# Workspace rounds of a six-stage transformer kernel: mean squares taken from the layer norm, the ends of two sequences alternating on VectorE, two sequences' final statistics by ScalarE's sums

## The reference, cut to what matters

```python
for _ in range(2):
    logits = _rms(x, norm_pre_w) @ compete_w.T + compete_b      # 16 slots
    vals, idx = jax.lax.top_k(jnp.swapaxes(logits, 1, 2), 4)
    wgt = jax.nn.softmax(vals, axis=-1)
    ...                                                          # gather, write, norm: ws
    q, kk, vv = x @ wq.T + bq, ws @ wk.T + bk, ws @ wv.T + bv    # by 8 heads
    att = jax.nn.softmax(jnp.einsum('blhd,bshd->bhls', q, kk) * scale, axis=-1)
    x_b = ctx @ out_proj_w.T + out_proj_b                        # ctx = att @ vv
    x = _rms(x + x_b, norm_post_w)
...
x = _layernorm(x + _L1_xattn_ref(x, ...))     # fifth
x = _layernorm(x + _L1_ffn_ref(x, ...))       # sixth, with the rounds above
```

## Time and profile before

| | before |
|---|---|
| median of three runs | 2493.07 us |
| profiled execution: its own time | 2491.76 us |
| profiled execution: span | 2490.0 us |
| TensorE, VectorE, ScalarE, GpSimd busy, share of the span | 87%, 57%, 51%, 41% |
| mean granted TensorE clock, share of 2.4 GHz | 0.951 |
| last stage | from 2222.6 us to the end |
| last VectorE instruction, last ScalarE instruction ends | 2482.3, 2485.29 |
| last store issued | 2485.31 |

### The profile page before, as it was taken

How to read it: one execution, slowest core, us unless ns; L and a number is a source line. 1 busy time by engine, 2 the same in 40 slices (tenths; PEclk the granted TensorE clock), 3 DMA queues, 4 the chain that set the end, 5 groups by cost and what they waited for, 6 DMA issues and landing times. The chain is left out here.

```text
span 2490.0 us, 33458 instructions
## 1 busy us (share of the span) xinstructions
PE 2164.6 (87%) x12629; PEld 1546.5 (62%) x12664; DVE 1423.2 (57%) x2130; ACT 1258.6 (51%) x2385; POOL 1017.3 (41%) x726
## 2 busy tenths in 40 slices
PE   5989898968896797787999999999999999977782
PEld 4555555536785666565777777777777777744340
DVE  3656666645555435543566765566556665552637
ACT  3636363633425636544555565556655565541413
POOL 2424252511003202203666666666666666530101
PEclk9999999988997999998999999999999999988796
DMA  3000000010001000002111111111111111020001
GB/s 113 1 1 1 1 1 1 1 64 1 1 1 50 1 1 1 1 2 78 51 51 51 60 51 51 47 47 47 48 51 52 51 51 52 18 70 31 1 1 68
DMA packets 60552, 79.14 MB, mean 32 GB/s; under 512 B 6052, under 2 KB 40228, under 8 KB 60392
## 3 DMA queue, kind: packets, MB, share of 16 engines
q1 hardware_dynamic: 60392, 76.99, 9.3%
HBM read 72.78 MB, written 4.19 MB: 31 GB/s over the span
## 5 line engine op out<-in xcount | busy, mean ns | idle before, releaser
L2133 PE MATMUL banks<-s_probsT,s_v 128*128 128x512 f32 x512 | 230.1, 592 | 0.0
L594 DVE TENSOR_REDUCE s_neg_max<-banks 128x1 f32<-128x512 f32 x256 | 165.5, 685 | 89.4 <-PE banks L660 88.0
L2039 DVE RECIPROCAL s_inv_sums<-banks 128x512 f32<-128x512 f32 x64 | 214.2, 3346 | 2.3 <-PE banks L2143 2.3
L1964 ACT ACTIVATE s_probsT<-banks,s_minus_bound,s_qk_rstd 128x512 f32<-128x512 f32 x256 | 186.4, 784 | 11.8 <-PE banks L200 11.8
L543 ACT ACTIVATE s_probsT<-banks 128x512 f32<-128x512 f32 x256 | 148.7, 600 | 81.4 <-PE banks L674 79.1
L1993 DVE TENSOR_REDUCE s_mean_sq<-x_cur 128x8 f32<-128x1024 f32 x64 | 78.1, 1220 | 184.9 <-ACT x_cur L1932 174.4
L1860 POOL TENSOR_TENSOR s_qk_rstd<-s_mean_sq,minus_half 128x8 f32<-128x8 f32 x64 | 105.1, 1642 | 145.8 <-DVE s_mean_sq L1996 142.5
L198 PE MATMUL banks<-s_w_proj_hi,xT_hi 128*128 128x256 f32 x512 | 157.9, 308 | 2.9 <-DVE s_w_proj_lo L2016 2.9
L2133 PEld LDWEIGHTS banks<-s_probsT,s_v 128*128 128x128 f32 x512 | 96.9, 189 | 97.6 <-issue 84.9
L482 POOL TENSOR_TENSOR x_cur<-s_probsT 128x512 f32<-128x512 f32 x64 | 82.0, 1282 | 158.3 <-PE banks L692 109.9
L200 PE MATMUL banks<-s_w_proj_hi,xT_lo 128*128 128x256 f32 x512 | 145.4, 284 | 0.0
(11 more groups left out here) (422 smaller groups left out, 6270.6 us busy)
## 6 DMA issues: line engine op xcount, KB each, us to landing
s_w_proj_raw<-l1x_wq SPq DMA_DIRECT2D x32, 512.0 KB, 3.4
s_w_out_raw<-l1x_wo SPq DMA_DIRECT2D x32, 512.0 KB, 3.6
s_w_proj_raw<-l1x_wk SPq DMA_DIRECT2D x32, 256.0 KB, 2.8
s_w_proj_raw<-l1x_wv SPq DMA_DIRECT2D x32, 256.0 KB, 3.0
x_all<-x SPq DMA_DIRECT2D x4, 1024.0 KB, 12.0
s_ctxT<-ctxT SPq DMA_DIRECT2D x8, 512.0 KB, 4.7
out<-x_all SPq DMA_DIRECT2D x4, 1024.0 KB, 4.3
s_probsT<-l0a_wqkv SPq DMA_DIRECT2D x1, 1536.0 KB, 9.6
```

The costliest lines, as they stand in the source:

```text
L594: dve.tensor_reduce(nmax[:, h % 2, t, 0:1], ps.ap(s), AX.X, ALU.max, negate=True) \
L1964: act.activation(probs[:, h, k, :], ps.ap(("E", j, h, k)), ACT.Exp, bias=bound[:, 0:1], scale=rs[:, 1, k, h:h + 1]).then_inc(ps.freed(("E" ...
L2039: dve.reciprocal(inv[:, h, :], ps.ap(("SU", j, h))).then_inc(ps.freed(("SU", j, h)), 1)
L2133: mm = pe.matmul(ps.ap(key), v[:, k, h * DX:(h + 1) * DX], probs[:, h, k, :], start=(k == 0), stop=(k == T - 1))
```

## The change

Four things are changed.

1. The layer norm at the end of the fifth stage leaves the mean square of its output, variance x rstd x rstd, in a new tile `x_mean_sq` (the output's mean is zero). The first round's Q phases use it, before the transposes; ScalarE's squares of the first round are gone, and the first round's transposes use banks 0, 1, 4 and 5 in turn. The competition weights have a semaphore of their own and are loaded second; VectorE scales them ahead of its first copy.
2. Between the rounds the squares are a phase of their own, `Xs`, placed behind the next transposes; the squares of sequence 2 are not made by ScalarE, but its mean square comes from VectorE's `bn_stats`, as variance + mean squared.
3. The end of the second round is split in phases that alternate between sequences: D (adding `xw` to x), for sequences 0 and 1 Ms (ScalarE's sums of the tiles), Mm (VectorE: minus mean), Mq (ScalarE's squares about the mean, with a sum), Mv (VectorE: variance + eps), for sequences 2 and 3 Mb (`bn_stats` and `bn_aggr` as before), F (shift) and O.
4. The last sequence is stored in four pieces of 256 KB, each when its tile is done.

Semaphores and helpers that were no longer used are removed.

```diff
+                    mean_sq = c.x_mean_sq[:, j * T:(j + 1) * T]
+                    dve.tensor_tensor(mean_sq, c.mv[:, :, 1], c.rstd[:, :], ALU.mult)
+                    dve.drain()
+                    dve.tensor_tensor(mean_sq, mean_sq, c.rstd[:, :], ALU.mult)
...
-        seq = [("X", 0, 0), ("X", 0, 1), ("Q", 0, 0), ("X", 0, 2), ("Q", 0, 1), ("X", 0, 3), ("Q", 0, 2), ("Q", 0, 3)]
+        seq = [("Q", 0, b) for b in range(B)] + [("X", 0, b) for b in range(B)]
         for r in range(R):
             def ph(*names, r=r):
                 return [(n.rstrip("0123"), r, int(n[-1])) for n in names]
...
             if r == 0:
-                seq += [*ph("N0", "C2", "R1"), ("X", 1, 0), *ph("B3", "Cs2", "N1", "C3", "R2"), ("Q", 1, 0)]
-                seq += [("X", 1, 1), *ph("Cs3", "N2", "R3"), ("Q", 1, 1), ("X", 1, 2), *ph("N3"), ("Q", 1, 2)]
-                seq += [("X", 1, 3), ("Q", 1, 3)]
+                seq += [*ph("N0", "C2", "R1"), ("X", 1, 0), *ph("Cs2", "B3", "N1", "R2", "C3"), ("X", 1, 1)]
+                seq += [*ph("Cs3", "N2", "R3"), ("Xs", 1, 0), ("X", 1, 2), ("Q", 1, 0), *ph("N3"), ("Xs", 1, 1)]
+                seq += [("X", 1, 3), ("Q", 1, 1), ("Xs", 1, 2), ("Q", 1, 2), ("Xs", 1, 3), ("Q", 1, 3)]
             else:
-                seq += ph("C2", "R1", "N0", "B3", "Cs2", "C3", "R2", "O0", "N1", "Cs3", "R3", "O1", "N2", "O2", "N3", "O3")
+                seq += ph("C2", "R1", "N0", "B3", "Cs2", "C3", "R2", "D0", "Cs3", "Ms0", "N1", "Mm0", "Mq0", "D1", "Mv0")
+                seq += ph("R3", "Ms1", "N2", "F0", "Mm1", "Mq1", "O0", "D2", "Mv1", "Mb2", "F1", "O1")
+                seq += ph("N3", "F2", "O2", "D3", "Mb3", "F3", "O3")
...
-                uses += [(("x", r, b, k), k % 2, 1) for k in range(KD)]
+                uses += [(("x", r, b, k), k % 2 if r else (0, 1, 4, 5)[k], 1) for k in range(KD)]
...
         def _(sp):
-            sp.dma_start(pre[:, :], d["l1f_pre"]).then_inc(small, 16)
+            sp.dma_start(pre[:, :], d["l1f_pre"]).then_inc(cw_in, 16)
+            sp.wait_ge(zeroed, 1)
+            sp.dma_start(cw[:, :, 0:NS], d["l1f_cwT"].rearrange("(k p) n -> p k n", p=P)).then_inc(cw_in, 16)
+            for b in range(B):
+                sp.dma_start(cb[b * SB:b * SB + NS, :], d["l1f_cb"]).then_inc(small, 16)
             for j, nm in enumerate(("l1f_bq", "l1f_bk", "l1f_bv")):
                 sp.dma_start(bqkv[:, j, :], d[nm]).then_inc(small, 16)
             for dst, nm in ((wb, "l1f_wb"), (post, "l1f_post"), (ob, "l1f_ob")):
                 sp.dma_start(dst[:, :], d[nm].broadcast_to([P, D])).then_inc(small, 16)
-            sp.wait_ge(zeroed, 1)
-            sp.dma_start(cw[:, :, 0:NS], d["l1f_cwT"].rearrange("(k p) n -> p k n", p=P)).then_inc(small, 16)
             for b in range(B):
-                sp.dma_start(cb[b * SB:b * SB + NS, :], d["l1f_cb"]).then_inc(small, 16)
                 sp.dma_start(ws[b * SB:b * SB + NS, :], d["l1f_ws"]).then_inc(small, 16)
             for dst, nm in ((ww, "l1f_wwT"), (wk, "l1f_wkT"), (wv, "l1f_wvT"), (wq, "l1f_wq"), (wo, "l1f_woT")):
                 sp.dma_start(dst[:, :, :], d[nm].rearrange("(k p) n -> p k n", p=P)).then_inc(large, 16)
-            for b in range(B):
+            for b in range(B - 1):
                 sp.wait_ge(*normed.after(b, T))
                 sp.dma_start(c.out[b].rearrange("(t p) d -> p t d", p=P), c.x[:, b * T:(b + 1) * T, :]).then_inc(stored, 16)
-            sp.wait_ge(stored, 16 * B)
+            for t in range(T):
+                sp.wait_ge(*normed.after(B - 1, t + 1))
+                sp.dma_start(c.out[B - 1, t * P:(t + 1) * P, :], c.x[:, (B - 1) * T + t, :]).then_inc(stored, 16)
+            sp.wait_ge(stored, 16 * (B - 1 + T))
...
-                elif ph == "O":
+                elif ph in ("Mv", "Mb"):
                     rstd(rstd_f, veps_f, var_ready, rstd_ready, b, cols)
...
-                    squared(source(r), ssq, b * T, None, x_sq)
+                elif ph == "Xs" and b != BY_VARIANCE:
+                    squared(xw, ssq, b * T, lambda t: xw_ready.after(b, t + 1), x_sq)
...
+                elif ph == "Ms":
+                    act.drain()
+                    for t in range(T):
+                        i = b * T + t
+                        act.wait_ge(*x_added.after(b, t + 1))
+                        s = act.activation(squares[t][:, :], c.x[:, i, :], ACT.Copy, accum_out=sum_f[:, i:i + 1])
+                    s.then_inc(sums_ready.sem, 1)
+                elif ph == "Mq":
+                    act.wait_ge(*nmean_ready.after(b, 1))
+                    act.drain()
+                    for t in range(T):
+                        i = b * T + t
+                        s = act.activation(squares[t][:, :], c.x[:, i, :], ACT.Square, bias=nmean_f[:, i:i + 1],
+                                           accum_out=ssq_f[:, i:i + 1])
+                    s.then_inc(sums_ready.sem, 1)
...
                 if ph == "X":
+                    if r == b == 0:
+                        dve.wait_ge(cw_in, 32)
+                        for k in range(KD):
+                            last = dve.tensor_scalar(cw[:, k, :], cw[:, k, :], pre[:, k:k + 1], None, ALU.mult)
+                        last.then_inc(cw_ready, 1)
                     for k in (1, 3):
                         dve.wait_ge(*ps.full(0, ("x", r, b, k)))
                         dve.tensor_copy(xT[b][:, k, :], ps.ap(("x", r, b, k))).then_inc(ps.freed(("x", r, b, k)), 1)
                 elif ph == "Q":
-                    mean(ms, ssq, cols, x_sq, x_ms, turn)
-                    if r == 0 and b == 0:
-                        dve.wait_ge(small, 16 * 16)
-                        dve.drain()
-                        for k in range(KD):
-                            last = dve.tensor_scalar(cw[:, k, :], cw[:, k, :], pre[:, k:k + 1], None, ALU.mult)
-                        last.then_inc(cw_ready, 1)
+                    if r == 0:
+                        dve.tensor_scalar(ms[:, cols], c.x_mean_sq[:, cols], EPS6, None, ALU.add).then_inc(x_ms.sem, 1)
+                    elif b != BY_VARIANCE:
+                        mean(ms, ssq, cols, x_sq, x_ms, b - (b > BY_VARIANCE))
+                elif ph == "Xs" and b == BY_VARIANCE:
+                    dve.drain()
+                    for i in range(b * T, (b + 1) * T):
+                        dve.bn_stats(stats_f[:, i, :], xw[:, i, :])
+                    dve.drain()
+                    for i in range(b * T, (b + 1) * T):
+                        dve.bn_aggr(mv_f[:, i, :], stats_f[:, i, :])
+                    dve.drain()
+                    dve.tensor_tensor(sq_mean[:, :], mv_f[:, cols, 0], mv_f[:, cols, 0], ALU.mult)
+                    dve.drain()
+                    dve.scalar_tensor_tensor(ms[:, cols], sq_mean[:, :], EPS6, mv_f[:, cols, 1], ALU.add, ALU.add).then_inc(x_ms.sem, 1)
                 elif ph == "S":
                     dve.wait_ge(*ps.full(0, ("L", r)))
                     dve.wait_ge(*ps.released(0, ("R", r)))
                     dve.wait_ge(zeroed, 1)
+                    dve.wait_ge(small, 16 * 14)
                     dve.drain()
                     dve.tensor_tensor(lrow[:, 0:S], ps.ap(("L", r)), rrow[:, :], ALU.mult).then_inc(ps.freed(("L", r)), 1)
                     dve.drain()
@@ -2514,22 +2539,31 @@
                     for i in tiles:
                         dve.scalar_tensor_tensor(xw[:, i, :], xw[:, i, :], rs_y[:, i:i + 1], post[:, :], ALU.mult, ALU.mult) \
                            .then_inc(xw_ready.sem, 1)
-                    if r == R - 1:
-                        dve.drain()
-                        for i in tiles:
-                            dve.tensor_tensor(c.x[:, i, :], c.x[:, i, :], xw[:, i, :], ALU.add)
-                        dve.drain()
-                        for i in tiles:
-                            dve.bn_stats(stats_f[:, i, :], c.x[:, i, :])
-                        dve.drain()
-                        for i in tiles:
-                            dve.bn_aggr(mv_f[:, i, :], stats_f[:, i, :])
-                        dve.drain()
-                        dve.tensor_scalar(veps_f[:, cols], mv_f[:, cols, 1], 1e-5, None, ALU.add).then_inc(var_ready.sem, 1)
-                elif ph == "O":
+                elif ph == "D":
+                    dve.drain()
+                    for i in range(b * T, (b + 1) * T):
+                        o = dve.tensor_tensor(c.x[:, i, :], c.x[:, i, :], xw[:, i, :], ALU.add)
+                        if ("Ms", r, b) in seq:
+                            o.then_inc(x_added.sem, 1)
+                elif ph == "Mm":
+                    dve.wait_ge(*sums_ready.after(b, 1))
+                    dve.tensor_scalar(nmean_f[:, cols], sum_f[:, cols], -1.0 / D, None, ALU.mult).then_inc(nmean_ready.sem, 1)
+                elif ph == "Mv":
+                    dve.wait_ge(*sums_ready.after(b, 2))
+                    dve.tensor_scalar(veps_f[:, cols], ssq_f[:, cols], 1.0 / D, 1e-5, ALU.mult, ALU.add).then_inc(var_ready.sem, 1)
```

(14 more changed lines are left out.)

37 lines of the change are left out of this document (11 added, 26 removed).

## The result

| | before | changed |
|---|---|---|
| median, us | 2493.38 (2491.44 to 2494.36, 4 runs) | 2472.39 (2470.48 to 2474.26, 4 runs) |
| ratio | | 0.9917 [0.9900, 0.9934] |
| profiled execution: own time, span | 2491.76, 2490.0 | 2470.48, 2468.7 |
| mean granted TensorE clock | 0.951 | 0.955 |
| last stage starts at (SyncE's first load of it) | 2222.63 | 2217.43 |

The changed kernel is faster by 0.8%, inside the predicted range. The last stage is 16.1 us shorter, where the prediction summed 15.8. Measured again beside other runs of the kernel before, the changed kernel had a ratio of 0.9932 [0.9920, 0.9945], so the gain is 0.7 to 0.8% by the two medians.

What follows compares the result with a forecast made beforehand. Bounds: ScalarE's squares with two banks (opening), TensorE (second opening), VectorE with GpSimd waits (tail). Terms -5.7 + 1.8 - 10.0 - 1.9 = -15.8 us give median 2477.3, forecast 2477; 8-in-10 range 2471.5 to 2483.

Steps and rivals of the forecast that it cites:

- The layer norm, 0: End of the stage before: two added VectorE operations of 128x4 per sequence cost 0; without cover 1.6 us.
- The opening, -5.7: First round's opening: squares removed and four banks bring the row product 5.7 us earlier; bounds 2.1 and 8.4.
- I take 7.1 us, half way: First opening: the eleven transpose groups left take 7.1 us, between 9.6 (lower clock) and 4.9 (upper).
- The -8.4 that stood as the bound: First opening: largest gain, 8.4 us, with weights landing after 1.9 us and all transposes at the upper clock.
- Rival A: First opening: TensorE stops for VectorE's wait, transposes stay at 1.2 GHz; only 2.1 us gained, 2481 us; chance 0.15.
- The second opening, +1.8: Second round's opening: sequence 2's late statistics and two serial rstds delay the row product 1.8 us; bounds 0 and 2.5.
- 1.5 us to either side: Elsewhere in the last stage: allowance of 1.5 us for products shifting against TensorE's clock changes.
- The tail, -10.0: End of second round: two statistics and idle waits leave VectorE's list, 10.0 us gained; bounds 9.0 and 11.2.
- four waits for GpSimd, 6.4 us: Tail: VectorE's idle waits of 2.1, 2.1, 1.1 and 1.1 us before the last variance all go.
- The small operations, put at 1.2 us net: Tail: eight added VectorE operations of 128x4, with drains, cost about 1.2 us net.
- Rival B: Tail: VectorE waits in order for ScalarE's sums; whole 15.8 us gain gone from 1.7 us per piece; chance 0.02.
- The store, -1.9: Last store: four of 256 KB, landing in 2.4 us against 4.3 for 1 MB, gain 1.9; bounds 1.0 and 2.4.

## Why the prediction was right, point by point

1. **What bounds each place** was read rightly: ScalarE's squares and two banks at the opening, TensorE at the second, VectorE with idle waits for GpSimd in the tail. Each part alone moved its own piece by about what the whole change moves it (8.0, 2.05, 10.1 us).
2. **The layer norm, 0:** held (0.9994, with an interval over 1).
3. **The opening, -5.7, was -7.8.** The load (2.40 for 2.4), VectorE's first copy (4.50 us into the stage for 4.57), the competition products (3.57 for 3.46) and the row product without a wait (0.92 for 0.93) held. The step that failed is "I take 7.1 us, half way" between all transposes at the upper and all at the lower level: the rest took 5.02 us, where 4.9 was the end of the range for all high. The reason given for the middle was the clock of 0.69 with waits in every group; but with four banks there is one stop of 0.89 and then none, and the clock had risen 0.4 us before it. The -8.4 that stood as the bound was nearly reached. What the prediction did not separate is the share of the banks: with the squares gone, 5.8 of the 7.8 us hang on them, as the run with two shows.
4. **Rival A** (transposes stay at 1.2 GHz) did not come true, and the rule of the Trainium skill, TensorE: Matmul & The Clock Gate, section HAM oscillation, as the prediction read it, would have put the opening at -2.1. In the changed kernel there are hardly any waits left between bursts. The section also speaks of another case than the prediction made of it: its example waits for transfers longer than its bursts last, and the clock falls in each wait. Even the kernel with two banks doesn't show that. There the clock was at the lower level from the stage's start on and stayed there for 10.4 us, over 36 transposes and a stop of 2.36 us (0.51 up to 2233.20), and then rose to 1.00 although stops of 0.18 to 0.35 us went on. It came up late; it didn't fall back.
5. **The second opening, +1.8, was +2.0** behind the last copy: VectorE 3.66 us for 3.4, two rstds 1.98 for 2.02, the row product 1.07 for 0.93. Another 0.27 us is lost ahead of the last copy: of the 1.0 in the table, 0.73 is there from the first 31 us of the stretch on, before any instruction that the edit moves. The +0.9 behind it was in no term of its own, but is of the kind for which it allowed 1.5 us to either side, products that shift against the clock: the gather's products took 5.57 us at 0.65 in place of 4.96 at 0.73. The run with the squares alone has 79.63 there too, and those with the layer norm or the tail alone 78.8, so the shift seems to come with this edit.
6. **The tail, -10.0, was -10.0,** but by two errors that cancel. The prediction took four waits for GpSimd, 6.4 us, out of VectorE's list up to the last variance. Only three stand in that list (2.10, 2.09 and 1.12, together 5.3). The fourth, 1.12 us at 2482.16, comes behind the last variance at 2481.04, and it is still there in the changed kernel, where none was forecast. The small operations, put at 1.2 us net, cost about 0.15: the list went from 39.62 to 29.67 us, and 9.95 is 6.0 and 5.3 less 1.2 of waits for ScalarE and 0.15. These waits, estimated 0.6 each, are 0.74 and 0.46; ScalarE's second pass takes 0.71 a piece, between the 0.70 and 0.73 named. The run with alternation alone bears this out: 5.05 us for the three waits of 5.3, and the sums 4.9. Rival B needed 1.7 us a piece. The rule of the Trainium skill, ScalarE: Activation LUTs, section Rules for kernel authors, that sends additions and products to VectorE gives its factor for bf16; in f32 ScalarE's pass takes 0.61 here, as the prediction read from the rows of before, and moving two statistics to ScalarE gained 4.9 us.
7. **The store, -1.9, was -2.25:** 256 KB land in 2.0 us where 2.4 was the estimate. One store of 1 MB gives 4.66 again.
8. **The sum.** -15.8 for -16.1 in the stage: the opening was 2.1 too small and the store 0.35, the second round's opening and the stretches before and behind it 2.1 too favourable. That the errors cancel is luck; and so, in part, is the tail, the largest term, which was right to 0.1 by the two errors of point 6. The median lies 4.6 below the forecast of 2477, nearly as much as executions of one kernel differ ahead of the stage; the second measurement of the same kernel gave 2474.5.

## What to carry to other kernels

Where an engine fills banks that two others empty, its stops can cost twice, as idle time (2.6 us here) and by a clock that stays down longer (1.5 us); ask how many banks are free before asking who is slow. A wait for a small load belongs behind the copies that free the producer, not ahead of them: the consumer of the loaded data is often much later. In a tail of one engine with short replies from another, let pieces of two sequences alternate, and count the idle waits up to one fixed event, since the last reply has nothing to hide behind; and before statistics move to another engine, take the price of its pass from a row of the same type and shape.

## What the runs showed of the hardware

- A stop of 0.89 us that began 0.4 us after TensorE's clock had risen did not send it down again; a stop of 2.36 us after 12 transposes at the lower level was followed by nearly 24 more at it, before the clock rose. Without a stop 64 transposes took 8.86 us.
- The same 32 gather products took 6.25 or 5.02 us by the granted clock (0.63 or 0.77 in the 8.9 us around them). The stretch at the lower level behind the first row product was 10.2 us long in ten profiles and 6.8 in four.
- GpSimd's power of 128x4 took 1.01 us alone, beside `bn_stats` and beside the addition L2545, and 1.35 to 1.51 beside VectorE's scaling of rows (L2540), three times in the tail. It was hidden each time. What does that was not tried: the scaling had begun before GpSimd's operation each time, while the addition and the statistics began 0.01 to 0.02 us after it, so the order may matter and not the kind of operation.
- Over eleven profiles with the same first five stages, the last stage starts up to 6.8 us apart, 0.27% of the kernel: more than the terms of the second opening and the store together.
